# Adjacency masks made by class on Pool and turned by DMA transposes, prefix matmuls behind the projection, features normalised first

## What is computed

```python
h = jnp.maximum(_layernorm(x, axis=-1), 0.0)
mask = adj != 0
scores = jnp.where(mask, -jnp.arange(N), neg_inf)
vals, idx = jax.lax.top_k(scores, 25)            # the first 25 neighbours
agg = jnp.where(valid, h[idx], neg_inf).max(axis=2)
agg = jnp.where(degree <= 25, jnp.maximum(agg, 0.0), agg)
out = relu(concat([h, agg]) @ W + b)             # W is 256 x 128
x = x + out
```

## Time and profile before

| | |
|---|---|
| median of three runs | 698.95 us (697.47 to 699.57) |
| profiled execution | 697.45 us, span of the instructions 695.7 us |
| mean granted TensorE clock | 0.993 of full speed |
| DMA | 67.6 MB, 97 GB/s on average |

### The profile page before, as it was taken

One profiled execution on the slowest core, in us unless ns is written; L12 is line 12 of the kernel. 1 busy time (PEld: TensorE's weight loads), 2 busy tenths in 40 slices (PEclk: granted clock), 3 DMA queues, 4 the chain that ended last, 5 costly groups with the idle time before them and its releaser, 6 DMA issues.

```text
span 695.7 us, 10819 instructions
## 1 busy us (share of the span) xinstructions
PE 630.9 (91%) x3376; PEld 297.4 (43%) x3376; DVE 613.7 (88%) x813; ACT 472.3 (68%) x642; POOL 50.3 (7%) x41
## 2 busy tenths in 40 slices
PE   2479998999989999899999999899999999999976
PEld 2133443535445354443545344353535335353423
DVE  3368999899998999989998899989998899988997
ACT  2689478783777639775795947777497927959120
POOL 1300021000210002100030002100021000300000
PEclk9899999999999999999999999999999999999999
DMA  9520141510415103251303313151122411020100
GB/s 361 199 87 27 60 152 68 182 70 16 152 73 200 60 15 136 83 188 60 128 23 122 151 60 151 68 196 57 41 122 87 185 60 32 16 107 1 60 15 16
DMA packets 19127, 67.64 MB, mean 97 GB/s; under 512 B 4499, under 2 KB 7830, under 8 KB 16534
## 3 DMA queue, kind: packets, MB, share of 16 engines
q1 hardware_dynamic: 19094, 67.26, 25.7%
HBM read 42.08 MB, written 4.19 MB: 67 GB/s over the span
## 4 chain that ended last, share of the span: by engine, by line
PE 66%; DVE 16%; issue 10%; ACT 4%; DVEq 1%; DMA 1%; POOL 1%; ACTq 0%
PE picked L506 18%; PE picked L507 17%; PE ring L455 14%; DVE late_hot L684 4%; PE side L469 4%; PE ring L449 4%; DVE hot L659 4%; PE side L463 4%; DVE best L775 3%; DVE best L678 3%; PE final L534 2%; PE final L538 2%; PE final L491 1%; DMA adj_in<-in_adj_dram 1%; DVEq L771 1%
## 5 line engine op out<-in xcount | busy, mean ns | idle before, releaser
L678 DVE TENSOR_TENSOR best<-picked,best 128x1024 f32<-128x1024 f32 x224 | 270.5, 1218 | 38.2 <-PE picked L507 36.0
L506 PE MATMUL picked<-hot,h_hi 128*128 128x512 f16 x512 | 194.5, 380 | 15.0 <-DVE best L775 7.5
L507 PE MATMUL picked<-hot,h_lo 128*128 128x512 f16 x512 | 194.0, 379 | 0.0
L506 PE MATMUL picked<-late_hot,hi_skew 128*128 128x512 f16 x336 | 127.6, 380 | 13.1 <-DVE late_hot L684 8.2
L507 PE MATMUL picked<-late_hot,lo_skew 128*128 128x512 f16 x336 | 127.3, 379 | 0.0
L344 ACT ACTIVATE late_rank<-ring,late_bias 128x512 bf16<-128x512 f32 x128 | 81.4, 690 | 57.6 <-PE ring L455 57.6
L775 DVE TENSOR_TENSOR best<-picked,best 128x1024 f32<-128x1024 f32 x84 | 102.4, 1219 | 8.3 <-PE picked L507 8.2
L378 ACT COPY best<-picked 128x1024 f32<-128x1024 f32 x32 | 32.2, 1013 | 102.6 <-PE picked L507 102.6
L659 DVE TENSOR_SCALAR hot<-rank 128x4096 f16<-128x4096 bf16 x64 | 89.4, 1399 | 12.0 <-ACT rank L344 12.0
L349 ACT ACTIVATE past<-side,bias_cut 128x512 bf16<-128x512 f32 x128 | 88.3, 690 | 6.2 <-PE side L469 4.9
L344 ACT ACTIVATE rank<-ring,bias_big 128x512 bf16<-128x512 f32 x128 | 83.1, 692 | 5.2 <-PE ring L455 4.9
(11 more groups left out here) (76 smaller groups left out, 562.1 us busy)
## 6 DMA issues: line engine op xcount, KB each, us to landing
adj_in<-in_adj_dram SPq DMA_DIRECT2D x16, 2048.0 KB, 7.7
late_skew<-late SPq DMA_DIRECT2D x32, 192.0 KB, 2.3
x_in<-in_x_dram SPq DMA_DIRECT2D x8, 512.0 KB, 8.5
xres<-in_x_dram SPq DMA_DIRECT2D x16, 256.0 KB, 7.8
late_skew<-late SPq DMA_DIRECT2D x16, 256.0 KB, 2.4
late_skew<-late SPq DMA_DIRECT2D x32, 128.0 KB, 2.0
out_dram<-xres SPq DMA_DIRECT2D x16, 256.0 KB, 2.0
late_skew<-late SPq DMA_DIRECT2D x32, 64.0 KB, 1.9
```

Of the source, the lines that this page charges most:

```text
L506: nc.tensor.matmul(dst, hi[:, slot, k, :], onehot, start=start, stop=False)
L507: return nc.tensor.matmul(dst, lo[:, slot, k, :], onehot, start=False, stop=stop)
L678: nc.vector.tensor_tensor(best[:, half, s, :, :], picked[s][:, :, :], best[:, half, s, :, :], ALU.max).then_inc(picked_read, 1)
```

## The change

- **Masks.** `mask` is laid out class by class, `[P, Q, K, P]`. For group 0 DVE makes it, for all later groups POOL, with `tensor_scalar` reading `adj_in` with a step of eight int32 and two `is_equal` with zero. ACT makes none.
- **Turning.** SP issues four DMA transposes (`dma_start_transpose`) for each group, 128 x 1024 bf16 each, from `mask` to `mask_t`, which has two slots now. PE's 32 transposes and ACT's four copies from `ring` are gone. POOL waits until the group before has been turned, and for the adjacency.
- **Order on PE.** The lower sums of group g + 2 stand behind the projection of g. The tables become `spread_over(4, 9), spread_over(4, 11), spread_over(9, 14)`; the late one-hots come behind uses 12 and 13 instead of 10 and 11, the count behind 11 instead of 9.
- **Start.** SP loads x before the adjacency of group 0, which comes in four pieces with their own semaphores; DVE makes statistics first and `make_gain` behind the first mask.

```diff
-    LATE_WITH, PREFIX_WITH, RANK_WITH = spread_over(5, 8), spread_over(5, 12), spread_over(9, 13)
-    LATE_HOT_USES, COUNT_USE, MASK_USES = (10, 11), 9, (4, 9)
+    LATE_WITH, PREFIX_WITH, RANK_WITH = spread_over(4, 9), spread_over(4, 11), spread_over(9, 14)
+    LATE_HOT_USES, COUNT_USE = (12, 13), 11
...
-    TURNS = K // 2
-    FIRST_RING = 2 * TURNS + K
-    RING = 2 * K + TURNS
+    FIRST_RING = K
+    RING = 2 * K
+    TURNED = 16 * Q
...
-        mask = sb("mask", [P, Q, N], BF16)
-        mask_t = sb("mask_t", [P, K, ROWS], BF16)
+        mask = sb("mask", [P, Q, K, P], BF16)
+        mask_t = sb("mask_t", [P, 2, K, ROWS], BF16)
...
+            def turn_masks(slot):
+                sp.reg_add(masks_due, masks_due, Q)
+                for q in range(Q):
+                    sp.wait_ge(mask_made, q + 1)
+                    if q == 0:
+                        sp.wait_ge(mask_made, masks_due)
+                    sp.dma_start_transpose(mask_t[:, slot, :, q * P:(q + 1) * P],
+                                           mask[:, q, :, :].rearrange("p k j -> p (k j)")).then_inc(mask_turned, 16)
...
-            load_adj(0, 0)
             load_x(0)
+            for q in range(Q):
+                sp.dma_start(adj_in[:, 0, q * N:(q + 1) * N], adj_v[0][:, q * N:(q + 1) * N]).then_inc(adj_first[q], 16)
             load_adj(1, 1)
...
             for g in (0, 1):
-                sp.wait_ge(mask_made, Q * (g + 1))
+                turn_masks(g)
                 load_adj(g + 2, g)
             skew_h(0, 0)
             skew_late(0)
...
                     load_x(batch_of(it, u) + 1)
+                if not at_end(it, u, 2):
+                    turn_masks(u % 2)
                 if not at_end(it, u, 1):
                     skew_late(g + 1)
...
+            def make_masks(slot):
+                pool.reg_add(turned_due, turned_due, TURNED)
+                pool.reg_add(adj_due[slot], adj_due[slot], 16)
+                pool.wait_ge(mask_turned, TURNED)
+                pool.wait_ge(mask_turned, turned_due)
+                pool.wait_ge(adj_loaded[slot], adj_due[slot])
+                for q in range(Q):
+                    nc.gpsimd.tensor_scalar(mask[:, q, :, :], adj_in[:, slot, q * N:(q + 1) * N].rearrange("p (j k) -> p k j", k=K),
+                                            0.0, 0.0, ALU.is_equal, ALU.is_equal).then_inc(mask_made, 1)
...
             normalize(0)
             low_part(0, 0)
+            make_masks(1)
             def step(it, u):
                 g = g_of(it, u)
+                if not at_end(it, u, 2):
+                    make_masks(u % 2)
...
-            def lower_sums(turned):
+            def lower_sums(g, half):
+                pe.wait_ge(mask_turned, TURNED * (g + 1))
                 for k in range(K):
-                    if k % 2 == 0:
-                        pe.wait_ge(ring_read, turned + k // 2 + 1)
-                    nc.tensor.matmul(side[:, :], before[:, :], mask_t[:, k, :], start=(k == 0), stop=(k == K - 1))
+                    nc.tensor.matmul(side[:, :], before[:, :], mask_t[:, half, k, :], start=(k == 0), stop=(k == K - 1))
...
-                    if use == PAIRS and more:
-                        lower_sums(at - TURNS)
...
-                if not at_end(it, u, 2):
-                    turn_mask(g + 2, at + TURN_AT, 0)
                 if more:
                     pick_pair(g + 1, 2, next_slot)
-                if not at_end(it, u, 2):
-                    turn_mask(g + 2, at + TURN_AT, 1)
-                if more:
                     pick_pair(g + 1, 3, next_slot)
-                if not at_end(it, u, 2):
-                    turn_mask(g + 2, at + TURN_AT, 2)
-                    turn_mask(g + 2, at + TURN_AT, 3)
                 project(g, it, u, new_batch)
+                if not at_end(it, u, 2):
+                    lower_sums(g + 2, u % 2)
```

100 lines of the change are left out of this document (37 added, 63 removed).

## The result

| | before | after |
|---|---|---|
| median | 698.21 us | 779.69 us |
| all runs | 697.45 to 699.57 (4) | 776.24 to 783.97 (4) |
| ratio, 95% interval | | 1.117 [1.111, 1.123] |
| span of the profiled execution | 695.7 us | 777.0 us |
| mean granted clock | 0.993 | 0.977 |

The change costs 81 us, where +29 was forecast. The side was right and the main cause is the one that was named, POOL's masks holding up DVE; the size was not right, and the time lies outside the range of 680 to 768. (The granted clock is TensorE's, as a share of full speed.)

A forecast was written before the change was run, and what follows sets the result against it. The prediction took DVE to set the pace, with PE's transposes hidden behind it. 697.45 - 4.6 (start) + 3 (tables) + 31 (POOL's masks) = 727 us, given as 728 for the median; range 680 to 768.

The forecast's parts named there:

- The transposes are hidden behind DVE.: PE beside DVE's tail up to take 3: removing 41.0 us of transposes gains almost nothing, since DVE runs there without gaps.
- When do they run.: POOL's masks in a step: they start at E + 15 to E + 17, or E + 24 with new features, among DVE's one-hots.
- How long is one?: One mask pass on POOL: 1.66 us, taken from affine_select, bounds 0.96 and 1.95; with the hold, +31 us over 14 groups.
- rival 1: POOL's masks: a strided pass is longer, 2.28 us, losing 64 us in all, 760 us (771 by the skill's figure); 13%.
- A one-hot waits until POOL's instruction is over.: DVE beside POOL's masks: each one-hot met waits for the pass to end, 0.52 us in lockstep, about 2.2 us a group.
- The tables: +3 us.: PE's new order up to take 10: 0.4 us gained in steps without new features, 0.8 lost in those with, +3 us.
- The start: -4.6 us.: Kernel's beginning with x first: first one-hot at 31.5, use 5 taken at 47.5; -4.6 us, between -2 and -9.
- SP: four transposes cost nothing: SP's queue in a step: four DMA transposes ahead of the late marks fit into 18 us, costing nothing at 4.5 us each.
- rival 4: DMA turning sets the pace: at 10.5 us a transpose a step takes 52 us, the kernel about 840 us; 5%.
- Rivals 2 and 3: POOL's masks don't hold one-hots: PE's waits disappear too, 677 us, 24%; or they come back at use 10, 696 us, 13%.

The follow-up runs named there:

- e2: The changed kernel with group 1's masks made by DVE instead of POOL, POOL still making those of group 2 and later: 768.6 us, 1.102.
- e7: The changed kernel with group 1's masks on DVE and later ones on ACT, a step sooner, in its gap at a step's end; new tables kept: 715.6 us.
- e9: e7 with the tables of the kernel before (late ranks, prefix sums, ranks, count and late one-hots at their old places): 691.5 us, 0.988.
- e8: The kernel before with the change's start alone: x first, group 0's adjacency in four pieces, statistics and gain around the first mask: 692.3 us, 0.991.
- e3: The kernel before plus four idle POOL passes of the change's strided form in each of 14 steps, on buffers nobody else uses: 751.8 us, 1.076.
- e3d: The kernel before plus the same idle POOL passes as e3, but reading and writing densely: 706.1 us, 1.010.

## Why the prediction was right in side and wrong in size

The three parts of the steps can be put together from the table. Masks on POOL rather than in ACT's gap: 664.4 - 616.2 = 48.2 us with the new tables, 642.5 - 594.5 = 48.0 with the old. New tables: 664.4 - 642.5 = 21.9 with POOL's masks, 616.2 - 594.5 = 21.7 without. What is left, transposes off PE and lower sums moved, with the masks in ACT's gap, is 594.5 - 603.2 = -8.7. Each of the two prices comes out nearly the same in both pairs, so they add: 48 + 22 - 9 = 61. The agreement to 0.2 us is closer than single executions warrant; by the medians the masks cost 64.1 and 67.6 us, start included, and the tables 20.5 and 24.1. The first group's 20.1 us are 12.5 for group 1's masks (e2), 4.4 for POOL's other passes (96.9 to 92.5), 1.3 for the tables (92.5 to 91.2) and 1.9 for the rest.

Against the prediction's own terms, the masks cost 48 us in the steps where 31 stood (17 missed), tables and freed PE together 22 - 9 = 13 where 3 stood (10 missed), and the start 20 where -4.6 stood (25 missed). These are the 52 us between +29 and +81. Behind the first and behind half of the third lies one step that failed, the length of a mask on POOL (1.66 us given, 5.0 measured), made milder in the first by an opposite error in the hold.

**"The transposes are hidden behind DVE."** Right. 41.0 us of PE's work went, and that with the lower sums' move is worth 8.7 us under the old tables. Take 4 waits 0.51 us in every second step (389.29), where 0.45 was worked out, and not at all in the others. The sign that was named for it came too: the waits behind the first group's end stayed about what they were and moved from use 5 to use 10.

**"When do they run."** Right within 2 us. POOL begins at 360.18. Take 3 ends as `finish_group` starts, so E is 342.7 and this is E + 17.5, where E + 15 to E + 17 was given. In steps with new features it is E + 25, where E + 24 was given. From then on the one-hots are met.

**"How long is one."** This is the step that failed most. I took 1.66 us from an affine_select, with 1.95 above as the bound. Measured are 4.6 us where DVE has no one-hot beside the pass and 5.0 in the mean, since DVE holds POOL back as well. The upper bound was a pass over two dense float tensors, and I let it stand for a strided read of int32 with two compares, although rival 1 said that no row had one. The runs take it apart: dense with two compares 4.08, strided with one 4.07, strided with two 5.0, strided write 8.1. So taking away the stride alone or the second compare alone leaves 4 us; a dense pass with one compare wasn't run, and why it is 4 us stays open. Nothing in the trace of before was near. Rival 1, at 13%, came nearest, with 2.28 us a pass and 760 us. That is in part luck, since it had 64 us for the holds, too much, and nothing for the start and the tables. The Trainium skill ("GPSIMD Engine Reference", "Performance pitfalls for Q7 kernels") pointed the right way, to an estimated 2.5 us and 771 us. The trace doesn't agree with the figure: the strided pass took twice that, and the dense one, which the same section has at about 1.9 cycles an element (an estimated 1.6 us), took 4.08.

**"A one-hot waits until POOL's instruction is over."** Wrong for these passes, and it made the forecast better than its parts, which is luck: with 4.6 us a pass, one-hots in lockstep would lose 4.6 - 1.14 = 3.5 us four times in a group, 14 x 14 = 196 us in all. Measured is a hold in parts of the pass: 1.7 to 1.9 us for a one-hot at its beginning, 0.7 behind that, none in its middle, 0.8 towards its end. The step shown meets it seven times, between 0.26 and 1.71 us, 6.2 us in all. Over the whole run the groups' means grew by 73 us; part of it is taken up by waits of the takes, 48 remain in the steps. My sum had 31, from a pass three times too short and a hold that was taken for the whole pass. Rows 5 could not tell the two apart: L303 takes 2.14 us, and each of the seven `hot` that begin 0.34 us into it loses 1.66 us. That fits a hold to its end as well as one of its first 2 us, like the one at the beginning of a strided read.

**"The tables: +3 us."** The two waits that I worked out are there, 0.51 at take 4 and 1.80 at take 10, which begins at E + 10.9 (E + 11.5 given). Against before, steps with new features are 0.8 to 0.9 us longer in e7 (40.0 between two `finish_group` in place of 39.1), as given (+0.8). But the steps without new features are 0.2 to 0.9 longer and not 0.4 shorter, and the last five intervals lose 5.9 together, so e7 is at +13.0 where +3 stood. What I missed is larger: I compared with the kernel before, where the transposes still stand on PE. With them gone, the lower sums moved and the tables left alone, 8.7 us were to be had, and the tables' real price is 22. The crowd before take 10 is made by the tables and not by the lower sums: in e9, which moves the lower sums too, take 10 never waits.

**"The start: -4.6 us."** Wrong, +15.1 at use 5 and +20.1 at the first `finish_group`. For the first one-hot 31.5 was given and it came at 36.96. The three masks ended at 15.1 (13.7 given), a strided one takes 1.08 us alone on DVE in place of 0.69, and turning took from 15.21 to 22.63, 7.4 us where I had put 3. Then group 1's masks, 18.9 us in place of four times 1.66, stood in front of the late marks. The order on SP was read rightly ("for these SP must have issued POOL-made masks' transposes"); the duration was the same wrong one. Two of its sums also don't close by some tenths (13.7 + 3 + 3 + 11.1 is 30.8 and not 31.5, 39.2 + 7 x 0.6 + 1.9 is 45.3 and not 45.8), which changes nothing. e8 shows that the idea of the start was worth 6.2 us with PE turning and dense masks.

**"SP: four transposes cost nothing", rival 4.** In the steps right: 2.8 us each in the mean on SP's queue (4.5 and 3.8 for the first two, beside the adjacency, and 1.3 for the others), done 7 us ahead of the late marks. PE's waits for them, 26.5 us in the row of L463, are 22.63 at group 0 and 3.9 at group 1, none in the steps. Rival 4 falls. (Its own sum is too high: four at 10.5 and 7.7 are 49.7 us and not 52.) The Trainium skill's 1309 ns for one block ("VectorE: DVE Perf Modes", "The three transpose paths") doesn't add up by blocks here: a transpose of eight blocks lands after a median of 3.4 us, where eight times 1309 ns would be an estimated 10.5. "As fast as regular DMAs", from the Trainium skill's "Advanced Engine Details and Errata" ("X-Bar Transpose (TRN2)"), is nearer but not met either: a plain copy of the same 256 KB (`late_skew`) lands after 2.4 us. No step was bound by them, although the number of packets rose from 19127 to 87140.

**Rivals 2 and 3** ("a mask on POOL, with one input, doesn't hold DVE's one-hots") fall by e3. For a dense mask they would have been nearly right (e3d).

**What stays open.** What POOL does in the parts of a pass in which it holds DVE, and why they lie elsewhere with other steps; why even the shorter passes take 4 us; whether a dense pass would stay so cheap if DVE's one-hots fell elsewhere in it; whether it is the side or the size of the step that made the strided write so dear; how the 8.7 us divide between the transposes and the lower sums; and why the new tables cost just 1.5 us a step (that it is waiting of the takes for PE is shown, which of the moved matmuls does it isn't). A dense mask on POOL in the change itself wasn't tried: its layout would undo the change.

## What to carry to other kernels

Work put on an idle engine isn't free because the engine is idle: ask which instructions of the busy engine it meets and at which point of its own, and price the delay of each. A duration must come from an instruction of the same operation, types and steps; where there is none, the sum has no upper bound from the neighbours, and one such instruction, put idle into the kernel before, settles price and side effect in one run. And of a change with several parts each should be priced with the others already made: here the freed PE time with the moved lower sums was worth 8.7 us, and the tables that came with them cost 22.
